# Node blocks of 128 rows in place of 125 in a two-layer graph network kernel

## The reference

```python
h = relu(layernorm(x))                       # layer 0: attention over edges, then a feed-forward
qkv = (layernorm(h) * ga + ba) @ Wqkv + bqkv # 3125 x 768, 8 heads of 32
scores = sum over d of (q*SCALE)[src] * k[dst]
sa = softmax of scores over the edges of one dst
agg = segment_sum(v[src] * sa, dst)
x1 = h + agg
x = x + x1 + gelu((layernorm(x1)*gr+br) @ W_in + b_in) @ W_out + b_out
h = relu(layernorm(x))                       # layer 1: relational convolution, 8 relations
W = einsum('rb,bio->rio', comp, basis)
msgs = (h @ W[r])[src, edge_type]
z = gelu(segment_sum(msgs, dst) + h @ loop_w + h_bias + h)
x = x + layernorm(z) * gamma + beta
```

## Time and profile before

| | |
|---|---|
| median of 3 runs | 1698.16 us (1694.78 to 1698.62) |
| the profiled execution's own time | 1690.69 us |
| its span, first to last instruction | 1688.6 us |
| PE busy | 1229.1 us (73%) |
| DVE busy | 973.0 us (58%) |
| POOL busy | 887.1 us (53%) |
| ACT busy | 388.5 us (23%) |
| DMA, mean of 16 engines | q0 (gathers) 30.7%, q1 (the other transfers) 18.0% |
| mean rate of the DMA engines | 151 GB/s |

### The profile page before, as it was taken

How to read it: one execution, slowest core, us unless ns; L and a number is a source line. 1 busy time by engine, 2 the same in 40 slices (tenths; PEclk the granted TensorE clock), 3 DMA queues, 4 the chain that set the end, 5 groups by cost and what they waited for, 6 DMA issues and landing times. The chain is left out here.

```text
span 1688.6 us, 25178 instructions
## 1 busy us (share of the span) xinstructions
PE 1229.1 (73%) x4992; PEld 832.7 (49%) x4992; DVE 973.0 (58%) x3071; ACT 388.5 (23%) x991; POOL 887.1 (53%) x934
## 2 busy tenths in 40 slices
PE   1567187888787878839999999993666776666773
PEld 0233066666665666626565655642444554444552
DVE  4455478888887888765455544231355454455554
ACT  1355133333332333223323232220000000000000
POOL 1730077777777777722122021014777777777771
PEclk9778699999999999969999999996787778788776
DMA  3533488888888888823212111123444444444441
GB/s 115 94 119 118 167 258 255 260 260 256 258 260 256 255 259 260 256 89 107 107 49 97 44 77 62 60 86 101 122 133 130 130 127 127 130 130 130 127 127 46
DMA packets 135072, 255.21 MB, mean 151 GB/s; under 512 B 38008, under 2 KB 84283, under 8 KB 131922
## 3 DMA queue, kind: packets, MB, share of 16 engines
q0 software_dynamic: 50176, 154.19, 30.7%
q1 hardware_dynamic: 84871, 100.76, 18.0%
HBM read 193.31 MB, written 61.57 MB: 151 GB/s over the span
## 5 line engine op out<-in xcount | busy, mean ns | idle before, releaser
L791 POOL DMA_INDIRECT arena<-qv_tab,arena x392 | 392.8, 1002 | 144.5 <-issue 126.9
L1393 POOL DMA_INDIRECT arena<-h_all,arena x392 | 376.3, 960 | 145.4 <-issue 104.5
L1462 PE MATMUL ps<-arena 128*128 128x256 f32 x784 | 275.1, 498 | 164.3 <-DMA arena<-h_all,arena 129.1
L1462 PEld LDWEIGHTS ps<-arena 128*128 128x128 f32 x784 | 180.5, 246 | 248.8 <-DMA arena<-h_all,arena 178.2
L895 PE MATMUL ps<-arena 128*128 128x264 f32 x800 | 234.1, 417 | 49.6 <-DVE arena L974 49.2
L884 PE MATMUL ps<-arena 128*128 128x264 bf16 x1188 | 174.7, 284 | 43.9 <-DVE arena L963 43.1
L986 DVE TENSOR_TENSOR arena<-arena,ps 128x512 f32<-128x512 f32 x196 | 134.3, 685 | 91.7 <-DMA arena<-qv_tab,arena 80.2
L895 PEld LDWEIGHTS ps<-arena 128*128 128x128 f32 x800 | 139.3, 194 | 96.8 <-DVE arena L974 57.1
L884 PEld LDWEIGHTS ps<-arena 128*128 128x128 bf16 x1188 | 140.5, 146 | 93.1 <-DVE arena L963 78.3
L1202 PE MATMUL ps<-wrel,arena 128*125 128x512 f32 x400 | 176.7, 595 | 5.3 <-ACT arena L1142 5.3
L1100 POOL COPY hs<-arena 125x256 f32 (+1 forms) x25 | 9.9, 396 | 271.2 <-ACT arena L1137 271.2
(11 more groups left out here) (171 smaller groups left out, 1499.0 us busy)
## 6 DMA issues: line engine op xcount, KB each, us to landing
h_all<-arena SPq DMA_DIRECT2D x25, 1000.0 KB
arena<-dst SPq DMA_DIRECT2D x51, 256.0 KB, 4.9
arena<-k_tab SPq DMA_DIRECT2D x50, 198.0 KB
att<-arena SPq DMA_DIRECT2D x51, 132.0 KB
rel<-arena SPq DMA_DIRECT2D x50, 128.0 KB
arena<-qv_tab,arena POOLq DMA_INDIRECT x392, 4.4
arena<-h_all,arena POOLq DMA_INDIRECT x392, 2.9
qv_tab<-arena SPq DMA_DIRECT2D x25, 250.0 KB
```

What stands on the lines that cost most here:

```text
L791: pool.indirect_dma_start(out=rowbuf[:, u * T + t, 0:2 * D], out_offset=None, in_=qv_tab, in_offset=bass.IndirectOffsetOnAxis(ap=idx[:, u, ...
L1393: pool.indirect_dma_start(out=rowbuf[:, u * T + t, :], out_offset=None, in_=h_all, in_offset=bass.IndirectOffsetOnAxis(ap=idx[:, u, t:t + ...
L1462: last = nc.tensor.matmul(ps[:, 6 + u, 0:D], ind[:, u, t, :], rowbuf[:, u * T + t, :], start=(t == 0), stop=False)
```

## The change

P is 128. The 25 blocks now cover 3200 rows (NP); the last one has 53 rows of nodes (LASTP), the rest of it is padding. The block count, the chunks and every loop stay as they are. The tables in DRAM grow to 3200 rows and more. The last block of x is loaded by a transfer of its own, after a memset that zeroes its place, and its result is stored with 53 rows.

```diff
-P = 125
-NBLK = N // P
+P = 128
+NBLK = -(-N // P)
+NP = NBLK * P
+LASTP = N - (NBLK - 1) * P
...
-NPAD = N + 3 * P
+NPAD = NP + 3 * P
...
-    qv_tab = nc.dram_tensor("qv_tab", (N, 2 * D), FP32).ap()
+    qv_tab = nc.dram_tensor("qv_tab", (NP, 2 * D), FP32).ap()
...
-    h_all = nc.dram_tensor("h_all", (N * R, D), FP32).ap()
+    h_all = nc.dram_tensor("h_all", (NP * R, D), FP32).ap()
...
-                sp.wait_ge(padded, 4)
+                sp.wait_ge(padded, 5)
...
-                sp.dma_start(xs_v[:, CH:NBLK, :], x_v[:, CH:NBLK, :]).then_inc(s_x, 16)
+                sp.dma_start(xs_v[:, CH:NBLK - 1, :], x_v[:, CH:NBLK - 1, :]).then_inc(s_x, 16)
+                sp.dma_start(xs_v[0:LASTP, NBLK - 1, :], x[N - LASTP:N, :]).then_inc(s_x, 16)
...
-                            act.wait_ge(s_x, 16)
+                            act.wait_ge(s_x, 32)
...
+                nc.vector.memset(xs[:, (NBLK - 1) * D:NBLK * D], 0.0).then_inc(padded, 1)
...
-                        dve.wait_ge(s_x, 16)
+                        dve.wait_ge(s_x, 32)
...
-                def store_block(m):
+                def store_block(m, rows=P):
...
-                    sp.dma_start(out[bass.ds(m * P, P), :], outb).then_inc(out_sem, 16)
+                    sp.dma_start(out[bass.ds(m * P, rows), :], outb[0:rows, :]).then_inc(out_sem, 16)
...
-                    store_block(m)
+                    store_block(m, P if m < NBLK - 1 else LASTP)
```

More of the change, by code:

```diff
@@ L83, in program @@
     rel = nc.dram_tensor("rel", (NPAD, D), FP32).ap()
-    h_all = nc.dram_tensor("h_all", (N * R, D), FP32).ap()
-    x_v = x.rearrange("(b p) d -> p b d", p=P)
-    out_v = out.rearrange("(b p) d -> p b d", p=P)
+    h_all = nc.dram_tensor("h_all", (NP * R, D), FP32).ap()
+    x_v = x[0:N - LASTP, :].rearrange("(b p) d -> p b d", p=P)
     ctx = ExitStack()
@@ L232, in _ @@
                 sp.wait_ge(zeroed, 2)
-                for c in range(N, NPAD, P):
+                for c in range(NP, NPAD, P):
                     sp.dma_start(att[c:c + P, :], zero[:, 0, :]).then_inc(z_out, 16)
@@ L250, in _ @@
                 sp.wait_ge(s_b, 48)
-                sp.wait_ge(z_out, 16 * (NCH + 2 * (NPAD - N) // P))
+                sp.wait_ge(z_out, 16 * (NCH + 2 * (NPAD - NP) // P))
             @block.gpsimd
@@ L656, in maxima_sync @@
                     sp.nop(nofuse=True)
-                sp.dma_start(mall, m_tab[0:N, :].rearrange("(b p) h -> p b h", p=P)).then_inc(mall_in, 16)
+                sp.dma_start(mall, m_tab[0:NP, :].rearrange("(b p) h -> p b h", p=P)).then_inc(mall_in, 16)
                 sp.wait_ge(mparts_ready, 1)
                 for c in range(3):
-                    sp.dma_start(k_tab[0:N, c * KW + D:(c + 1) * KW].rearrange("(b p) h -> p b h", p=P),
+                    sp.dma_start(k_tab[0:NP, c * KW + D:(c + 1) * KW].rearrange("(b p) h -> p b h", p=P),
                                  mparts[:, c, :, :]).then_inc(shifts_out, 16)
```

## The result

The kernel after takes 1638.24 us (median of 4 runs, 1632.06 to 1642.63) against 1697.08 us for the kernel before on the same chip (4 runs, 1694.78 to 1698.62): a ratio of 0.9652, 95% interval [0.9615, 0.9689]. The forecast was 1637 us. The profiled execution took 1635.64 us with a span of 1633.7, against 1690.69 and 1688.6.

A forecast was written before the change was run, and what follows sets the result against it. The prediction took waits for 125-row transfers, on five of sixteen DMA engines, as what 128 rows would relieve. Its terms summed to -61.0 us: 1629.7 against the profiled 1690.7, 1637 against the median 1698.2; range 1616 to 1661.

The forecast's parts named there:

- The rate, on which everything rested: DMA transfers: 125 rows use five engines (share about 0.33), 128 rows use sixteen (0.94, 294 GB/s).
- Rest of x: Stage 1, DVE's wait for the remaining x blocks: L424 starts at 28 instead of 47.4, -19.4 us (-16 to -20).
- first chunk: Stage 1, first L462 to that of the second chunk: the table-store wait goes, -8.5 us (0 to -12).
- The crowded front: Rival, stage 1: edge lists hold the queue longer, second chunk starts late, 8.5 us less gain, 1646; chance 0.14.
- The other chunks: Stage 1, later chunks: 22.7 us each instead of 25.1, PE and ACT setting the pace, -8 us (-2 to -24).
- All waits are gain: Rival, stage 1 chunks: PE kept busy holds its upper clock, up to 16 us more gain, 1621; chance 0.10.
- Into stage 2: Gap from DVE's stage 1 end to stage 2: 21.8 becomes 3.3, -18.5 us (-10 if weights delay gathers, to -19).
- Stage 2, the term set at nothing: Stage 2 and the way to stage 3's first load: no change, 0 us.
- Stage 3: First att load 7.8 to 4.7, -3.2 us; gap into stage 4, -8.2 us through faster, unqueued message stores.
- the rival of slow stores: Table and message stores: 16 engines store under about 130 GB/s, 22 us less gain in parts 8, 9, 5, 1659; chance 0.10.
- the +3.3 of the columns: PE's L1174 and four kinds of turn stream 2.4% more columns where PE is the bound: +3.3 us (+2 to +4).
- The last store: End of the program: the 53-row result store takes 2.3 us on one engine instead of 1.1, +1.2 us (-1 to +2).

The follow-up runs named there:

- the first group of runs: Kernels with P of 126 and 127, and the kernel after with x or table transfers cut into 125 and 3 rows; kernel before there 2061.15 us.

## Why the prediction was right

**The rate, on which everything rested.** Right, and shown from three sides: 0.07 with 127 rows, 0.33 with every 128-row transfer cut at 125, up to 1.03 with 128. Two readings around it were loose. The share does not stand at three tenths through all of stage 1 before: slice 2 reads five, at 94 GB/s. And a mean of 0.33 while all engines work does not show a backlog, since the kernel after has the same mean; the ten microseconds in which nothing but stores ran did.

**Rest of x and first chunk.** -18.9 and -9.1 for -19.4 and -8.5. Two misses cancel in it: the issue came at 13.31, 4.7 us earlier, where 3 was estimated, but from there 15.2 us passed until the data was there at 28.49, where some 13 were taken (the issue of the last block alone took 6.11 us; the engines moved 252 GB/s from 14 to 28 us, and 294 was taken). L427 waits 0.49 us for it, so DVE's earlier work would have let it start at 28.0 at best. The crowded front did not come about: at 59.12 no wait stands before L465.

**The other chunks.** -8.7 for -8.0, which owes something to luck. 22.7 us a chunk was right only on the mean: 24.1, 23.2 and 21.5. In the sum, 13.4 us stand for the way from the first to the fifth L462, and the rows give 14.3 (112.35 to 126.67); the last chunk gave 2.3 us where 1 was taken. And two more profiles of the kernel after have -7.2 and -2.3 for the same term, the last near the bound of -2, because their second chunk or a later one is longer (last section). PE is who DVE waits for now, as said. "All waits are gain" did not come about: 23.2 us of waits for PE are left, at a granted clock of 0.86 in the second chunk and 0.93 from 105 to 125 us.

**Into stage 2.** The gap is 5.0 us, not 3.3. The prediction had the last table store land near DVE's end. It is issued at 146.44, only 0.7 us before that end at 147.13, and SP waits for it until about 148.8, 1.7 us past the end; this is what was missing. The three weight loads that SP issues in between, up to 148.43, cost little: they fill time in which it would wait for the store anyway. SP's wait for that store is 0.4 us in the kernel after, and 1.5 and 1.8 us in the two kernels that issue no weights there, whose gaps are 4.6 and 4.8 us.

**Stage 2, the term set at nothing.** This is the one step that failed, by 6 us in this profile, of which 2.8 have a cause that was shown. The bound of -10 in the term before had named the mechanism, the weights' 2.3 MB in front of the first gathers, and I chose its other end. The first gather follows 5.0 us behind the memset in place of 2.1, +2.8, and both kernels without weights in flight there gave 2.0 and 2.1. The other 3.8 us, from first to last gather 514.9 for 511.2, are not a cost that can be told from spread: nine profiles with 128 rows show 510.3 to 521.0, three of them of the kernel after itself 514.9, 515.1 and 510.3.

**Stage 3.** -3.4 for -3.2, -9.3 for -8.2 (a store of 1 MB lands after 3.9 us, where 5.1 was worked out from the rate of the weight loads; with this the rival of slow stores is out, since 1 MB in 3.9 us is 269 GB/s), and +1.8 for the +3.3 of the columns: the large group grew by 1.3 us where 2.4% of it are 2.2.

**The last store.** +1.4 for +1.2: 53 rows do fall to one engine. This term did use the rule on the engines, though the prediction says that its sum would be the same without it.

Against before's own time the sum was 6 us too large (-61.0 for -54.9). The distance of the medians is -58.8, so the median was met within 1.3 us. That closeness is partly luck: nearly 4 of the 6 us vanish because the profiled execution of the kernel before lay 6.4 us below its median and that of the kernel after only 2.6.

## What to carry to other kernels

If a profile's DMA share stands flat at a simple fraction (0.33, 0.07) while a queue has a backlog, look at the number of rows of its transfers before anything else, and cut the stretch fine enough to see that it stands flat: the mean alone proves nothing. The number of rows of a block is to be chosen for its factors and not only for what divides the data: 128 with a padded last block beats an exact 125 by 3.5% here, and a ragged tail of 53 rows is better stored as 48 and 5 (2.3 us in the traces). What an exact, narrow store costs shows only where someone waits for it: the same five engines were worth 9 to 10 us at the end of stage 3 and nothing in its body.

## What was not expected of the hardware

**Stage 1 has two courses with the same code.** DVE's end of stage 1 was 147.1, 148.5 and 153.7 us in three profiles of the kernel after, and 4.5 of the 6.6 us between the first and the last of them lie in one place: the second chunk, 24.1 us in one and 28.6 in the other. Of the other profiles with 128 rows and wide table stores, two have the short second chunk and four the long one. The groups of L449, L476, L467 and PE's L370 between 59 and 83 us, in the profile at 147.1:

```profile
L370 PE MATMUL ps<-arena 128*128 128x512 f32 (+1 forms) x40 | 15.8, 547 | 3.4 <-ACT arena L309 3.4
...
L449 DVE TENSOR_SCALAR arena<-hs,mvb,rsb 128x256 f32 x5 | 2.4, 537 | 0.1
...
L476 DVE TENSOR_TENSOR arena<-arena 128x256 f32<-128x256 f32 x5 | 2.3, 453 | 0.0
...
L467 DVE TENSOR_TENSOR arena<-ps,arena 128x256 f32<-128x256 f32 x5 | 2.1, 413 | 0.0
```

and in the one at 153.7:

```profile
L370 PE MATMUL ps<-arena 128*128 128x512 f32 (+1 forms) x35 | 16.6, 630 | 5.3 <-ACT arena L309 5.3
...
L449 DVE TENSOR_SCALAR arena<-hs,mvb,rsb 128x256 f32 x5 | 4.2, 912 | 0.1
L476 DVE TENSOR_TENSOR arena<-arena 128x256 f32<-128x256 f32 x5 | 4.1, 816 | 0.0
...
L467 DVE TENSOR_TENSOR arena<-ps,arena 128x256 f32<-128x256 f32 x5 | 2.1, 413 | 0.0
```

POOL works through both stretches, at the relation weights. L449 and L476, which read no PSUM, take 1.7 and 1.8 times as long in the second; L467, which reads PSUM, stays at 413 ns; in the chunk after, with POOL through, L449 takes 411 ns. PE, fed later, then runs at a granted clock of 0.79 instead of 0.86 in that stretch. By the Trainium skill (page "SBUF — State Buffer", section "Who interferes with whom"), DVE and GpSimd share one pair of ports, which only one of them holds at a time; a tensor_tensor with both inputs in SBUF, such as L476, needs its reading side, and a tensor_scalar, such as L449, where it runs in a mode that uses both port pairs. The trace agrees for L476 (816 ns for 453) and for L467, whose input from PSUM leaves it at 413 ns; that L449 runs in such a mode is not shown here. That the order in which the two meet is what chooses the course was not tried.

**The gather stages can be longer by 30 to 40% with nothing else changed.** In the first group of runs the four profiles show some 720 and 645 us from the first to the last gather of the two gather stages, in place of 510 to 521 and 495, with the slices of stage 2 at 180 GB/s for 257 (182 with 127 rows) and POOL waiting for ACT's indices (L794, 215.9 us in 45 pieces in the kernel with 126 rows, 3.4 in the kernel after). The granted clock from first to last gather of stage 2 was 0.81 in the kernel with 126 rows and 0.99 in the kernel after. The body of stage 3 kept its time (but for 127 rows). The kernel before was not profiled in that group; its own time was longer by as much. The ratios of this group are nearer to 1 in part because the same gain is divided by a longer time. The cause is open.
